# Second attention: the order of two TensorE steps changed, and the scaling of the row maxima moved from VectorE to ScalarE

## The chip, the cores and the metric

The kernel runs on one NeuronCore of a Trainium2 chip. The metric is the device time of one execution in microseconds. Five engines work side by side and wait for one another through semaphores: TensorE (PE, with its weight loads PEld), VectorE (DVE), ScalarE (ACT), GpSimd (POOL) and SyncE (SP), which issues most DMAs.

## The reference, cut to what matters

The program is a two-layer decoder over 128 sequences of 64 tokens of width 128. The change touches one of its stages, the self-attention of the second layer. It attends across the batch: for each of the 64 token positions ("columns") the 128 sequences are rows, with 16 heads of width 8, a bias key and value appended, and a relative position bias that a gate computed from the query scales.

```python
attn_weights = jnp.einsum('bth,bsh->bts', q, k)          # q scaled by hd**-0.5 / 32
gate = jax.nn.sigmoid((query_layer @ grep_w + grep_b).sum(-1, keepdims=True))
gate = (gate * grep_a).reshape(bsz * nh, tgt_len, 1)
attn_weights = attn_weights + gate * pb
probs = jax.nn.softmax(attn_weights, axis=-1)
attn = jnp.einsum('bts,bsh->bth', probs, v)
return attn @ out_w + out_b                              # then + x and a layernorm
```

## The kernel before, in words

The program runs its stages one after the other, with a barrier between them. `phase_attn1` is the stage in question. It handles 64 columns of 128 rows; four buffers of each kind let several columns be under way at once. `pipelined` writes the order of work out by hand: every engine walks the columns in the same rhythm, each column in four quarters (a = 0 to 3, four heads each), and in every quarter an engine runs a fixed list of steps that belong to different columns: `ahead2` and `ahead1` are the columns two and one further on, `column` the one whose scores are being made, `behind1` to `behind3` the ones before. The lists are the functions named `step`, one for each engine. An engine never leaves the order of its list, so a wait holds up all that stands behind it.

The way of a column: TensorE turns x (`turn_x`) and projects it (`project`, L1697 and L1698); VectorE adds the biases (L1894, L1896, L1900) and ends the column's rows with `choose` (L1905); ScalarE and GpSimd split them into float16 high and low parts (L1804 to L1806, L1660, L1661); VectorE transposes all in 32x32 blocks (`turn_rows`, L1910, 1.8 us each); GpSimd makes the gate's right-hand side (L1632); TensorE makes gates and values (`gates_and_values`, 4 matmuls on L1707 and 16 on L1709); ScalarE starts the sigmoid and copies the values (L1811, L1813, L1814), VectorE inverts it (L1915), GpSimd scales it (L1638).

Then come the quarters. TensorE makes four heads of scores (L1719). VectorE's `bias` adds the gated positions while it copies the scores out (L1930), takes the row maxima of four heads (L1932), and multiplies these by -SCALE (L1934, 128x4 values, after a wait for L1932's own end). ScalarE's `exps` waits for that, and computes exp(SCALE * score + negmax) for each head (L1820). TensorE turns the result (`turn`, L1727), ScalarE copies it (L1825), TensorE weighs the values (`weigh`, 32 matmul records on L1746), ScalarE copies that (`copy_weighed`, L1833), and TensorE combines the parts (`combine`, L1756 and L1758). VectorE's `normalise` (L1940, L1942) waits for `combine`; it stands in quarter 0 behind `bias` of the column two further on. Then TensorE turns and projects the result (L1764, L1768), VectorE adds x and takes the statistics (L1948, L1950, L1953), GpSimd makes the power (L1622 to L1627) and ScalarE the norm (L1848) and the store.

In quarter 0 TensorE's list reads: scores(column, 1), turn(behind1, 2), turn_x(ahead2), gates_and_values(ahead1), combine(behind2). In quarter 1 it goes on with project(ahead2), scores(column, 2), turn(behind1, 3) and turn_attn(behind2). In quarters 2 and 3 it has scores(column, 3), turn(column, 0), output(behind2), then scores(ahead1, 0), turn(column, 1), turn_last(behind1), weigh(behind1).

ScalarE's list in quarter 0 reads: copy_weighed, exps(behind1, 3), copy_turned, place_last, copy_x, gates_and_values, norm; then exps(column, 0) in quarter 1, exps(column, 1) and high_parts in quarter 2, exps(column, 2) in quarter 3.

Of the kernel before, what the change touches and what calls it, by code (L numbers as in the profile page):

```python
# [9 lines left out]
ACT = mybir.ActivationFunctionType  # L10
ALU = mybir.AluOpType
AX = mybir.AxisListType.X
# [1470 lines left out]
def phase_attn1(nc, w, x3, x4):  # L1483
# [11 lines left out]
    SCALE = HD ** -0.5 / 32.0  # L1495
# [4 lines left out]
    with Phase(nc, "c") as ph:  # L1500
        def slots(name, shape, dt=F32):
            return [ph.sb(f"{name}{j}", shape, dt) for j in range(U)]
# [8 lines left out]
        sc, pT = slots("sc", [T, H, KEYS]), slots("pT", [T, H, T])  # L1511
        top, negmax, den = slots("top", [T, H]), slots("negmax", [T, H]), slots("den", [T, H])
# [9 lines left out]
        names = ("consts", "xT_ready", "xT_copied", "qvk_ready", "vlast_ready", "whole_ready", "high_ready", "rows_ready", "misc_ready", "gate_exp", "v_ready",  # L1522
                 "gate_done", "posg_ready", "scores_ready", "biased", "top_ready", "exp_ready", "pT_ready", "pT_copied", "last_placed", "kv_next_ready",
                 "lastT_ready", "lastT_copied", "pv_ready", "attn_ready", "attnT_ready", "attnT_copied", "out_ready", "x_biased_ready", "x_added", "mv_ready",
                 "rstd_ready", "offset_ready", "x4_ready", "own_front", "var_ready", "gate_added", "gate_ready", "last_bias_ready", "gate_inverted", "own_quarters", "own_back", "waited", "pool_waited", "low_ready", "rhs_ready", "chosen_ready", "weighed_ready", "weighed_copied")
        (consts, xT_ready, xT_copied, qvk_ready, vlast_ready, whole_ready, high_ready, rows_ready, misc_ready, gate_exp, v_ready,
         gate_done, posg_ready, scores_ready, biased, top_ready, exp_ready, pT_ready, pT_copied, last_placed, kv_next_ready,
         lastT_ready, lastT_copied, pv_ready, attn_ready, attnT_ready, attnT_copied, out_ready, x_biased_ready, x_added, mv_ready,
         rstd_ready, offset_ready, x4_ready, own_front, var_ready, gate_added, gate_ready, last_bias_ready, gate_inverted, own_quarters, own_back, waited, pool_waited, low_ready, rhs_ready, chosen_ready, weighed_ready, weighed_copied) = (ph.sem(n) for n in names)

        def nth(it, j):
            return U * it + j + 1

        def quarter(it, j, a):
            return Q * U * it + Q * j + a + 1

        def slot(j):
            return j % U
# [27 lines left out]
        def run(part, position, *more):  # L1566
            if position is not None:
                part(*position, *more)
# [15 lines left out]
        with nc.Block() as block:  # L1584
            @block.sync
            def _(sp):
                def body(it):
                    for j in range(U):
                        if not is_first(it):
                            sp.wait_ge(xT_ready, nth(it, j) - U)  # L1590
                        sp.dma_start(x_sb[j][:], x3_tokens[bass.ds(U * it + j, 1)].rearrange("o r i d -> (o r) i d")).then_inc(loaded[j], 16)
                        if not is_first(it):
                            sp.wait_ge(x_biased_ready, nth(it, j) - U)
                        sp.dma_start(x_rows[j][:], x3_rows[bass.ds(U * it + j, 1)].rearrange("o h t d -> (o h) t d")).then_inc(rows_loaded[j], 16)
                peeled(nc.sync, steps, body)
                for j in range(U):
                    sp.wait_ge(stored[j], 16 * (steps + 1))
# [85 lines left out]
            def _(pe):  # L1683
# [86 lines left out]
                def step(a, ahead2, ahead1, column, behind1, behind2, behind3):  # L1770
                    if a == 0:
                        run(scores, column, 1)
                        run(turn, behind1, 2)
                        run(turn_x, ahead2)
                        run(gates_and_values, ahead1)
                        run(combine, behind2)
                    if a == 1:
                        run(project, ahead2)
                        run(scores, column, 2)
                        run(turn, behind1, 3)  # L1780
                        run(turn_attn, behind2)
                    if a == 2:
                        run(scores, column, 3)
                        run(turn, column, 0)
                        run(output, behind2)
                    if a == 3:
                        run(scores, ahead1, 0)
                        run(turn, column, 1)
                        run(turn_last, behind1)
                        run(weigh, behind1)  # L1790
                pipelined(nc.tensor, step)

            @block.scalar
            def _(act):
# [21 lines left out]
                def exps(it, j, a):  # L1816
                    s = slot(j)
                    act.wait_ge(top_ready, quarter(it, j, a))
                    for h in range(4 * a, 4 * a + 4):
                        last = nc.scalar.activation(sc[s][:, h, :], sc[s][:, h, :], ACT.Exp, bias=negmax[s][:, h:h + 1], scale=SCALE)  # L1820
                    last.then_inc(exp_ready, 1)
# [55 lines left out]

            @block.vector
            def _(dve):
                front_own, quarters_own, back_own = Own(dve, own_front), Own(dve, own_quarters), Own(dve, own_back)  # L1880
                dve.wait_ge(consts, 1)
                for j in range(U):
                    nc.vector.tensor_copy(gate_rhs[j][:, :, 0:4], w["gate_w"][:].unsqueeze(1).to_broadcast([P, 4, 4]))
# [3 lines left out]
                def place(it, j):  # L1887
                    return U * it + j
# [32 lines left out]
                    nc.vector.tensor_tensor(sc[s][:, :, T].rearrange("p (a i) -> p i a", a=4), gates_part(1), by_gate(last_bias[s]), ALU.add).then_inc(gate_done, 1)  # L1921

                def bias(it, j, a):
                    s, own, hs = slot(j), quarters_own, slice(4 * a, 4 * a + 4)
                    if a == 0:
                        own.step(place(it, j))
                        dve.wait_ge(gate_done, nth(it, j))
                    dve.wait_ge(scores_ready, quarter(it, j, a))
                    dve.wait_ge(posg_ready, quarter(it, j, a))
                    nc.vector.tensor_tensor(sc[s][:, hs, 0:T], sbank[a % 2][:], posg[a][:], ALU.add).then_inc(biased, 1)  # L1930
                    dve.wait_ge(biased, quarter(it, j, a))
                    m = own.mark(nc.vector.tensor_reduce(top[s][:, hs], sc[s][:, hs, :], AX, ALU.max))  # L1932
                    own.wait(m)
                    nc.vector.tensor_scalar(negmax[s][:, hs], top[s][:, hs], -SCALE, None, ALU.mult).then_inc(top_ready, 1)  # L1934

                def normalise(it, j):
                    s, own = slot(j), back_own
# [17 lines left out]
                def step(a, ahead2, ahead1, column, behind1, behind2, behind3):  # L1955
                    if a == 0:
                        run(bias, column, 0)
                        run(normalise, behind2)
                    if a == 1:
                        run(bias, column, 1)  # L1960
                        run(invert_gates, ahead1)
                        run(project, ahead2)
                    if a == 2:
                        run(bias, column, 2)
                        run(last_score, ahead1)
                        run(choose, ahead2)
                        run(add_x, behind2)
                    if a == 3:
                        run(bias, column, 3)
                        run(turn_rows, ahead2)  # L1970
# [841 lines left out]
def program(nc, d, out):  # L2812
# [10 lines left out]
    with Phase(nc, "all") as top:  # L2823
        ident = make_ident(nc, top)
        with Phase(nc, "w0") as ph:
            w = setup_l0(nc, ph, inputs("attn0"), ident)
            with Phase(nc, "parts") as parts:
                xT_parts = [parts.sb(f"xT_{part}", [D, TOK], F16) for part in ("high", "low")]
                phase_max(nc, d["xT"], w["Wkp"], w, xT_parts)
                phase_performer(nc, w, d["x"], xT_parts, y1)  # L2830
            phase_feed_forward0(nc, w, d["x"], y1, x1)
        with Phase(nc, "w2") as ph:
            w = setup_cross0(nc, ph, inputs("cross0"), ident)
            phase_cross0(nc, w, x1, d["ctx"], d["ctxT"], x3)
        with Phase(nc, "w3") as ph:
            w = setup_attn1(nc, ph, inputs("attn1"), ident)
            phase_attn1(nc, w, x3, x4)
        with Phase(nc, "w4") as ph:
            w = setup_cross1(nc, ph, inputs("cross1"), ident)
            phase_cross1(nc, w, x4, d["ctxT"], x5, x5T, coefT)  # L2840
        with Phase(nc, "w5") as ph:
            w = setup_moe(nc, ph, inputs("moe"), ident)
            phase_moe(nc, w, x5, x5T, coefT, out)
# [71 lines left out]
```

## Time and profile before

| | us |
|---|---|
| median of three runs | 4170.33 (4169.57 to 4176.07) |
| the profiled execution's own time | 4170.93 |
| its span | 4169.2 |
| the stage in question, from the profile's lines | about 1640 to 2515 |

Over the whole span TensorE is busy 85% of the time, VectorE 75%, ScalarE 56%, GpSimd 44%. These are averages over the stages with different limits; what follows reads the one stage. The span and the own time differ by 1.7 us of start and end. An instruction's row gives its start from the beginning of the span and its length. Two instructions of one engine that do not need each other overlap by about 0.1 us in the records, so start-to-start distances are what adds up.

### The profile page before, as it was taken

To read this page: it belongs to the slowest core of one execution; us is meant where nothing else is said; L and a number is where in the kernel's file an instruction comes from. 1 tells how busy PE (TensorE), PEld (TensorE's weight loads), DVE (VectorE), ACT (ScalarE), POOL (GpSimd) and SP (SyncE) were. 2 spreads that over 40 slices of the span, in tenths; PEclk is the share of its full clock that TensorE was granted. 3 is DMA by queue.
4 is the path that set the end of the run, shared out by engine and by line. 5 is a ranking of instruction groups with operands and counts; after the bars stand their busy time and mean duration, and the time that the engine had idled before them with its cause. 6 is when DMAs were issued, how large, how long until landed. Compare 5 with 4: busy or idle time off the path is not lost. (4 is left out here: it accounts for less than half of the span.)

```text
span 4169.2 us, 92263 instructions
## 1 busy us (share of the span) xinstructions
PE 3546.1 (85%) x30947; PEld 2307.8 (55%) x30947; DVE 3141.0 (75%) x6490; ACT 2355.2 (56%) x5257; POOL 1843.5 (44%) x2322
## 2 busy tenths in 40 slices
PE   6899999997776853899889996887849999999998
PEld 3466666664445752666666665776724444444443
DVE  6677777775664653888888885888858888888887
ACT  1455555555663431777777775556545555555555
POOL 1000000002654642655565662222237878787876
PEclk9999999998886775777776768889869999999999
DMA  2000000001112212000000001222165656655663
GB/s 79 7 9 10 10 10 10 10 10 31 54 38 76 68 37 41 16 13 15 14 14 15 14 9 49 57 55 56 46 159 141 135 136 139 134 142 134 138 135 88
DMA packets 279447, 245.68 MB, mean 59 GB/s; under 512 B 57832, under 2 KB 205196, under 8 KB 279180
## 3 DMA queue, kind: packets, MB, share of 16 engines
q1 hardware_dynamic: 270092, 239.77, 23.7%
q10 hardware_dynamic: 9216, 4.20, 0.4%
q8 instruction: 70, 1.15, 0.1%
q14 instruction: 69, 0.57, 0.0%
HBM read 210.34 MB, written 33.55 MB: 58 GB/s over the span
## 5 line engine op out<-in xcount | busy, mean ns | idle before, releaser
L2647 POOL TENSOR_TENSOR d_hidden<-d_gated,d_upper 128x512 f32<-128x512 f32 x528 | 801.9, 1544 | 228.7 <-DVE d_upper L2756 101.1
L2763 DVE TENSOR_TENSOR d_h_low<-d_hidden,d_h_high 128x512 f16<-128x512 f32 x528 | 540.8, 1024 | 118.8 <-ACT d_h_high L2723 117.5
L2717 ACT ACTIVATE d_gated<-d_g 128x512 f32<-128x512 f32 x528 | 315.2, 597 | 461.9 <-PE d_u L2663 461.9
L750 POOL MEMSET f_minus_half<- 128x4 f32 x1 | 0.1, 101 | 864.4 <-POOLq L37 864.4
L2756 DVE TENSOR_TENSOR d_upper<-d_u,d_coef 128x512 f32<-128x512 f32 x512 | 349.1, 682 | 29.3 <-DMA d_coef<-coefT 10.9
L2723 ACT ACTIVATE d_h_high<-d_hidden 128x512 f16<-128x512 f32 x528 | 328.4, 622 | 8.2 <-POOL d_hidden L2647 8.2
L1820 ACT ACTIVATE c_sc<-c_sc,c_negmax 128x129 f32<-128x129 f32 x1024 | 326.2, 393 | 11.8 <-issue 7.6
L1648 POOL TENSOR_TENSOR c_posg<-w_pos,c_gate 128x512 f32<-128x512 f32 x256 | 266.0, 1039 | 0.0
L2661 PE MATMUL d_g<-d_x_high,w_Wg_high 128*128 128x512 f16 x528 | 200.5, 380 | 72.0 <-POOL d_x_low L2640 36.8
L1825 ACT ACTIVATE c_pT<-c_turned 128x512 f32<-128x512 f32 x256 | 149.7, 585 | 153.8 <-PE c_turned L1727 153.6
L1727 PE MATMUL c_turned<-all_ident,c_sc 128*128 128x128 f32 x1024 | 229.7, 365 | 6.4 <-ACT c_sc L1820 5.9
L2661 PE MATMUL d_o<-d_h_high,w_Wd_high 128*128 128x512 f16 x528 | 200.1, 379 | 2.0 <-ACT d_h_high L2723 1.6
L2661 PE MATMUL d_u<-d_x_high,w_Wu_high 128*128 128x512 f16 x528 | 200.6, 380 | 0.0
L2663 PE MATMUL d_g<-d_x_low,w_Wg_high 128*128 128x512 f16 x528 | 200.6, 380 | 0.0
L2662 PE MATMUL d_g<-d_x_high,w_Wg_low 128*128 128x512 f16 x528 | 200.6, 380 | 0.0
L2662 PE MATMUL d_u<-d_x_high,w_Wu_low 128*128 128x512 f16 x528 | 200.4, 380 | 0.0
L2663 PE MATMUL d_u<-d_x_low,w_Wu_high 128*128 128x512 f16 x528 | 200.4, 379 | 0.0
L2662 PE MATMUL d_o<-d_h_high,w_Wd_low 128*128 128x512 f16 x528 | 200.1, 379 | 0.0
L2663 PE MATMUL d_o<-d_h_low,w_Wd_high 128*128 128x512 f16 x528 | 200.1, 379 | 0.0
L1727 PEld LDWEIGHTS c_turned<-all_ident,c_sc 128*128 128x128 f32 x1024 | 149.1, 183 | 63.3 <-issue 50.8
L1932 DVE TENSOR_REDUCE c_top<-c_sc 128x4 f32<-128x516 f32 x256 | 176.9, 691 | 8.8
L1719 PE MATMUL c_scores<-c_rows 24*128 24x128 f16 x1024 | 160.8, 290 | 19.4 <-DVE c_sc L1930 19.3
(409 smaller groups left out, 9909.5 us busy)
## 6 DMA issues: line engine op xcount, KB each, us to landing
d_coef<-coefT SPq DMA_DIRECT2D x256, 512.0 KB, 7.6
d_cT<-in_ctxT SPq DMA_DIRECT2D x128, 64.0 KB, 2.0
mx_x<-in_xT SPq DMA_DIRECT2D x16, 256.0 KB, 2.7
b_x<-in_x SPq DMA_DIRECT2D x64, 64.0 KB, 1.8
y<-b_y SPq DMA_DIRECT2D x64, 64.0 KB, 1.6
f_y<-y SPq DMA_DIRECT2D x16, 256.0 KB, 3.2
f_x<-in_x SPq DMA_DIRECT2D x16, 256.0 KB, 3.7
x<-f_res SPq DMA_DIRECT2D x16, 256.0 KB, 2.4
```

The source lines that it names most:

```text
L1648: nc.gpsimd.tensor_tensor(posg[a][:], w["pos"][:, hs, :], gate[s][:, hs].unsqueeze(2).to_broadcast([T, 4, T]), ALU.mult).then_inc(posg_rea ...
L1727: last = nc.tensor.transpose(tbank[a % 2][:, i, :], sc[slot(j)][:, 4 * a + i, 0:T], w["ident"][:])
L1820: last = nc.scalar.activation(sc[s][:, h, :], sc[s][:, h, :], ACT.Exp, bias=negmax[s][:, h:h + 1], scale=SCALE)
L1932: m = own.mark(nc.vector.tensor_reduce(top[s][:, hs], sc[s][:, hs, :], AX, ALU.max))
L2647: nc.gpsimd.tensor_tensor(hidden[b][:], gated[b][:], upper[b][:], ALU.mult).then_inc(h_ready, 1)
L2661: nc.tensor.matmul(out, weights[0], high, start=start, stop=False)
L2662: nc.tensor.matmul(out, weights[1], high, start=False, stop=False)
L2663: return nc.tensor.matmul(out, weights[0], low, start=False, stop=stop)
L2717: nc.scalar.activation(gated[b][:], ps_g[i][:], ACT.Silu, scale=1.0 / W_SCALE).then_inc(silu_ready, 1)
L2723: nc.scalar.activation(h_high[b][:], hidden[b][:], ACT.Copy).then_inc(h_high_ready, 1)
L2756: nc.vector.tensor_tensor(upper[b][:], ps_u[i][:], coef[c % CBUFS][:, u % CU, :], ALU.mult).then_inc(upper_ready, 1)
L2763: nc.vector.tensor_tensor(h_low[b][:], hidden[b][:], h_high[b][:], ALU.subtract).then_inc(h_low_ready, 1)
```

## The change

Two edits in `phase_attn1`.

TensorE, quarter 0: `combine(behind2)` now runs ahead of `gates_and_values(ahead1)`.

VectorE no longer multiplies the maxima by -SCALE: L1934 and the wait in front of it are gone, and L1932 itself releases ScalarE. ScalarE does the multiplication at the head of `exps`, one small copy for each quarter, and waits for its end before the four exponentials. A semaphore for VectorE's own quarters is replaced by one for ScalarE's.

```diff
                         run(turn_x, ahead2)
+                        run(combine, behind2)
                         run(gates_and_values, ahead1)
-                        run(combine, behind2)
...
                 def exps(it, j, a):
                     s = slot(j)
                     act.wait_ge(top_ready, quarter(it, j, a))
+                    nc.scalar.activation(negmax[s][:, 4 * a:4 * a + 4], top[s][:, 4 * a:4 * a + 4], ACT.Copy, scale=-SCALE).then_inc(negmax_ready, 1)
+                    act.wait_ge(negmax_ready, quarter(it, j, a))
                     for h in range(4 * a, 4 * a + 4):
...
                     dve.wait_ge(biased, quarter(it, j, a))
-                    m = own.mark(nc.vector.tensor_reduce(top[s][:, hs], sc[s][:, hs, :], AX, ALU.max))
-                    own.wait(m)
-                    nc.vector.tensor_scalar(negmax[s][:, hs], top[s][:, hs], -SCALE, None, ALU.mult).then_inc(top_ready, 1)
+                    nc.vector.tensor_reduce(top[s][:, hs], sc[s][:, hs, :], AX, ALU.max).then_inc(top_ready, 1)
```

## Rows read from the trace of the kernel before

**Rows 1.** The page: the span.

```profile
span 4169.2 us, 92263 instructions
```

**Rows 2.** Stretches: us; busy PE, PEld, DVE, ACT, POOL; clock; DMA. Then L1910 alone.

```profile
1668.05:2486.05 818.00, 740.15 (x6208) 546.98 (x6200) 700.08 (x1440) 596.54 (x1982) 488.38 (x899) 0.71 0.05 14
...
1668.05:2000.00 331.95, 44.97 (x25) 0.73 0.05 14
2000.00:2486.05 486.05, 62.93 (x35) 0.71 0.05 14
```

**Rows 3.** Waits from 1700 to 2500: total us, times, longest.

```profile
DVE c_den L1940 <- PE c_back L1758: 70.8, 59, 1.8
```

**Rows 4.** Timeline, VectorE in a short column: start us, us, instruction.

```profile
2008.96 1.80 DVE L1910 STREAM_TRANSPOSE c_rows<-c_padded 128x1568 f16<-128x1568 f16 x1
...
2011.37 0.69 DVE L1932 TENSOR_REDUCE c_top<-c_sc 128x4 f32<-128x516 f32 x1
...
2012.10 0.40 DVE L1934 TENSOR_SCALAR c_negmax<-c_top 128x4 f32<-128x4 f32 x1
...
2013.15 0.26 DVE L1940 RECIPROCAL c_den<-c_back 128x16 f32<-128x16 f32 x1 [0.65 <-PE c_back L1758]
...
2014.36 0.69 DVE L1932 TENSOR_REDUCE c_top<-c_sc 128x4 f32<-128x516 f32 x1
...
2015.17 0.24 DVE L1915 RECIPROCAL c_gate<-c_gate 128x16 f32<-128x16 f32 x1
...
2015.33 0.49 DVE L1894 TENSOR_TENSOR c_whole<-c_front,w_qvk_b 128x384 f32<-128x384 f32 x1
...
2020.41 0.69 DVE L1932 TENSOR_REDUCE c_top<-c_sc 128x4 f32<-128x516 f32 x1
...
2021.14 0.84 DVE L1934 TENSOR_SCALAR c_negmax<-c_top 128x4 f32<-128x4 f32 x1
...
2021.89 1.80 DVE L1910 STREAM_TRANSPOSE c_rows<-c_padded 128x1568 f16<-128x1568 f16 x1
```

**Rows 5.** Timeline, the other engines around quarter 0.

```profile
2010.73 0.41 PE L1690 MATMUL c_front<-all_ident,c_x 128*128 128x128 f32 x1
...
2011.80 0.49 PE L1756 MATMUL c_back<-c_vlast_rows,c_lastT 128*128 128x144 f32 x2
...
2012.13 0.98 PE L1758 MATMUL c_back<-w_picked,c_weighed 128*128 128x36 f32 x8
...
2020.91 1.04 POOL L1648 TENSOR_TENSOR c_posg<-w_pos,c_gate 128x512 f32<-128x512 f32 x1
...
2021.98 0.59 ACT L1833 ACTIVATE c_weighed<-c_back 128x512 f32<-128x512 f32 x1
...
2024.11 0.29 PE L1707 MATMUL c_misc<-c_gate_rhs,c_rows 128*128 128x8 f16 x4 [1.52 <-POOL c_gate_rhs L1632]
```

**Rows 6.** Timeline, the long column that follows.

```profile
2027.22 0.26 DVE L1940 RECIPROCAL c_den<-c_back 128x16 f32<-128x16 f32 x1 [1.79 <-PE c_back L1758]
...
2029.50 0.56 DVE L1894 TENSOR_TENSOR c_whole<-c_front,w_qvk_b 128x384 f32<-128x384 f32 x1
...
2036.35 1.80 DVE L1910 STREAM_TRANSPOSE c_rows<-c_padded 128x1568 f16<-128x1568 f16 x1
```

**Rows 7.** Timeline, TensorE's next `gates_and_values`, one column after that of rows 5.

```profile
2038.50 0.30 PE L1707 MATMUL c_misc<-c_gate_rhs,c_rows 128*128 128x8 f16 x4
```

**Rows 8.** Busy time by stretch, three stretches with their granted clock (PEclk).

```profile
2024.65:2038.30 13.65, 13.65 (x91) 10.15 (x90) 10.93 (x24) 8.60 (x28) 7.33 (x15) 0.50 0.05 14
2011.11:2024.11 13.00, 10.82 (x104) 7.91 (x104) 11.69 (x25) 10.39 (x36) 8.22 (x16) 0.87 0.05 15
...
2017.82:2021.23 3.41, 3.41 (x41) 2.42 (x38) 3.12 (x10) 2.37 (x8) 1.72 (x4) 0.50 0.00 0
```

**Rows 9.** Timeline, ScalarE: a small activation that waits for the one before.

```profile
2011.98 0.29 ACT L1811 ACTIVATE c_gate<-c_misc,w_neg_gate_b 128x16 f32<-128x16 f32 x1
...
2012.30 0.21 ACT L1813 ACTIVATE c_gate<-c_gate 128x16 f32<-128x16 f32 x1
```

More of the change, by code:

```diff
@@ L1524, in phase_attn1 @@
                  "lastT_ready", "lastT_copied", "pv_ready", "attn_ready", "attnT_ready", "attnT_copied", "out_ready", "x_biased_ready", "x_added", "mv_ready",
-                 "rstd_ready", "offset_ready", "x4_ready", "own_front", "var_ready", "gate_added", "gate_ready", "last_bias_ready", "gate_inverted", "own_quarters", "own_back", "waited", "pool_waited", "low_ready", "rhs_ready", "chosen_ready", "weighed_ready", "weighed_copied")
+                 "rstd_ready", "offset_ready", "x4_ready", "own_front", "var_ready", "gate_added", "gate_ready", "last_bias_ready", "gate_inverted", "negmax_ready", "own_back", "waited", "pool_waited", "low_ready", "rhs_ready", "chosen_ready", "weighed_ready", "weighed_copied")
         (consts, xT_ready, xT_copied, qvk_ready, vlast_ready, whole_ready, high_ready, rows_ready, misc_ready, gate_exp, v_ready,
@@ L1528, in phase_attn1 @@
          lastT_ready, lastT_copied, pv_ready, attn_ready, attnT_ready, attnT_copied, out_ready, x_biased_ready, x_added, mv_ready,
-         rstd_ready, offset_ready, x4_ready, own_front, var_ready, gate_added, gate_ready, last_bias_ready, gate_inverted, own_quarters, own_back, waited, pool_waited, low_ready, rhs_ready, chosen_ready, weighed_ready, weighed_copied) = (ph.sem(n) for n in names)
+         rstd_ready, offset_ready, x4_ready, own_front, var_ready, gate_added, gate_ready, last_bias_ready, gate_inverted, negmax_ready, own_back, waited, pool_waited, low_ready, rhs_ready, chosen_ready, weighed_ready, weighed_copied) = (ph.sem(n) for n in names)
         def nth(it, j):
@@ L1879, in _ @@
             def _(dve):
-                front_own, quarters_own, back_own = Own(dve, own_front), Own(dve, own_quarters), Own(dve, own_back)
+                front_own, back_own = Own(dve, own_front), Own(dve, own_back)
                 dve.wait_ge(consts, 1)
@@ L1923, in bias @@
                 def bias(it, j, a):
-                    s, own, hs = slot(j), quarters_own, slice(4 * a, 4 * a + 4)
+                    s, hs = slot(j), slice(4 * a, 4 * a + 4)
                     if a == 0:
-                        own.step(place(it, j))
                         dve.wait_ge(gate_done, nth(it, j))
```

## The prediction, made before the changed kernel was run

> **What bounds the kernel now.** I read the page first, for the span [rows 1], and found the stage by its lines. It is one stage of several, and the barrier behind it passes on whatever it gains or loses, so only its own rhythm matters. The busy time of its steady part comes next [rows 2]: VectorE runs L1910 once a column, 25 + 35 = 60 times in 818.0 us, so a column takes 13.63 us. In it TensorE is busy 740.15/60 = 12.3 us, VectorE 11.7, ScalarE 9.9, GpSimd 8.1. The granted clock is 0.71 on average, a mix of the levels 1.2 GHz (0.5) and 2.4 GHz (1.0): 42% of the time at the upper one.
>
> No engine is full, so the bound is a chain. The view of waits shows one wait of VectorE for another engine that counts: L1940 for TensorE's `combine`, 70.8 us in 59 times, 1.20 us a column [rows 3]. The timeline shows VectorE working without another such gap. From L1910 to L1910 a short column takes 2021.89 - 2008.96 = 12.93 us with 0.65 us of that wait [rows 4]; the column after it takes 2036.35 - 2021.89 = 14.46 with 1.79 us of it [rows 6]. Half the columns are of either kind, which makes the mean.
>
> Why `combine` is late shows on TensorE's side: it stands behind `gates_and_values`, which can only begin when L1910 and then GpSimd's L1632 are done. TensorE sits idle for that, 1.52 us before L1707 at 2024.11 [rows 5], although all that `combine` needs (ScalarE's L1833) was finished at 2021.98 + 0.59 = 2022.57. So the loop that sets the pace is: L1910, L1632, gates and values, `combine`, `normalise`, the rest of VectorE's list, L1910 again.
>
> **First edit, `combine` first.** Nothing is added; on TensorE two steps change places and SP's and GpSimd's queues are not touched. `combine` now waits for L1833 alone and takes 13.11 - 11.80 = 1.31 us at the upper clock level [rows 5]; in the long column it took until 2027.2 [rows 6]. VectorE wants it at the end of L1932, 2011.37 + 0.69 = 2012.06, or 3.10 us after L1910 started. From 2022.6 it would be done at 2023.9 to 2024.1, two microseconds after L1910's start: the wait of L1940 is gone in the columns that begin like this one. In the short column TensorE reached this place only at about 2011.0 (`turn_x` at 2010.73 for 0.41 us [rows 5]), so `combine` ends at 2012.3, 0.2 to 0.3 us late. At the lower clock level it takes about 1.1 us more, by the two waits (1.79 against 0.65 us [rows 4, 6]). What stands behind it pays: `gates_and_values` starts when `combine` ends, at worst 1.3 us later. Of that, VectorE's L1915 notices nothing, since it is not due until 2.9 us after L1940's place, and the transfer of the wait goes to `project`, next on TensorE, which L1894 needs.
>
> **Second edit, VectorE's part.** L1934 costs differently by the quarter. In quarter 0 L1932 ends at 2012.06 and L1934 at 2012.50: 0.44. In quarter 1 L1932 ends at 2015.05 and L1915 starts at 2015.17: 0.12, and quarter 2 repeats it. In quarter 3 L1932 ends at 2021.10 and L1910 starts at 2021.89: 0.79 [rows 4]. The long ones end when a GpSimd instruction ends: L1648 at 2020.91 + 1.04 = 2021.95, L1934 at 2021.98 [rows 5]. All of it lies on VectorE's chain. Together 0.44 + 0.12 + 0.12 + 0.79 = 1.47 us, and with the wait of 0.65 the short column shrinks from 12.93 to 10.8 us. That is VectorE's floor. I cost the next instructions at no new stall, since none of their kinds (reduce, transpose, reciprocal) shows varying lengths.
>
> **Second edit, ScalarE's part.** Four small copies a column. The trace of before has no 128x4 copy here; the nearest are L1813 (128x16, 0.21 us), and the pair L1811 and L1813, where the second waits for the first: 0.32 start to start for a length of 0.29 [rows 9]. Neighbours that don't wait overlap by nearly 0.1 us (L1915 ends at 2015.41, L1894 starts at 2015.33 [rows 4]). From below a copy costs 0.21 - 0.08 = 0.13 us, from above 0.21 + 0.03 = 0.24; since the exponentials must wait for its end I take 0.24, 4 x 0.24 = 1.0 us a column. ScalarE goes from 9.9 to 10.9 us a column. The Trainium skill, "ScalarE: Activation LUTs", section "What ACT_TABLE_LOAD costs", gives 186 ns plus 0.833 ns an element for such an instruction, an estimate of 0.19 us. By that figure the four would be 0.1 us a column cheaper than the 0.21 of the row; the small difference stays in the range.
>
> ScalarE waits long enough in a column (13.63 - 9.9 = 3.7 us) to take 1.0 in, as long as a column is longer than about 11.0 us. Queued behind the new wait are the exponentials, `copy_turned` and, from quarter 3, L1833. Who waits: `turn` and `combine` on TensorE. Against that, L1932 releases ScalarE 0.2 to 0.9 us sooner than L1934 did, so the exponentials do not come later.
>
> **What is late next.** By walking the two columns: the short one becomes 10.8 + 0.2 = 11.0. In the long one `combine` begins about 1.5 us sooner (TensorE's idle time is filled), so `project`, for whose end L1894 started at 2029.50 [rows 6], ends about 2028.0; VectorE wants it at L1910 plus the distance of the short column less what is gone in between, 2015.33 - 2008.96 - 0.44 - 0.65 - 0.12 = 5.16, so at 2027.05. It waits 0.9: 11.7 us. The mean of the two is 11.35.
>
> TensorE may not follow, and this decides. With the clock at 0.50 it was busy without a gap for 13.65 us (2024.65 to 2038.30) [rows 8], and from gates to gates, 2024.11 [rows 5] to 2038.50 [rows 7], took 14.39: a column at the lower level costs 14.4 us. The stretch 2011.11 to 2024.11 holds 10.82 us of work, 3.41 of it at 0.50 (2017.82 to 2021.23) [rows 8]. These 3.41 do 3.41/14.39 = 0.237 of a column, the other 7.41 us the remaining 0.763: a column at the upper level costs 9.7. With today's 42% of the time at the upper level a TensorE that never waits needs 1/(0.42/9.7 + 0.58/14.39) = 12.0 us. With 50% it is 11.6, with 60% 11.15.
>
> I expect the share to rise a little, since the idle gap before L1707 goes away (the clock fell at 2024.65, right behind it), and some waits to stay: 11.8 us a column. **The sum:** 60 x (13.63 - 11.8) = 110 us, and about 3 us for the columns at the two ends. The profiled execution's own time is 4170.9 us, 0.6 above the median of the three runs; 4170.9 - 113 = 4058 us.
>
> **Rivals.**
>
> 1. The clock stays up. The forecast then meets the floors of VectorE (10.8) and ScalarE (10.9 plus a stall or two): 11.0 to 11.2 us, 60 x 2.5 + 4 = 154 us less, 4017. For it: the gap before L1707 goes. Against: the clock stood at 0.50 through 13.65 us of unbroken work [rows 8], so a busy TensorE alone does not raise it here. The rule that speaks for this rival is in the Trainium skill, "TensorE: Matmul & The Clock Gate", section "Why this matters for your kernels": keep TensorE busy and free of long gaps and it holds full clock. By that rule the time would be this rival's 4017; the row just named disagrees. Chance 0.2.
>
> 2. The waits only move. `combine` waits for L1833 behind a fuller ScalarE, `gates_and_values` and `project` wait behind `combine`, and L1894 inherits most of L1940's wait. VectorE keeps the 1.47 us of L1934 at best, and half of it if TensorE's chain is the tighter: 12.3 to 13.0 us a column, 40 to 80 us less, about 4110. For it: the order of the work ahead of `project` is the same sum as before. Against: 1.5 us of idle time in half of the columns. Chance 0.2.
>
> 3. Slower: the clock stays at the lower level. The upper stretches of today begin near `weigh` and last through `combine` and `project`; if TensorE now waits for L1833 where it used to go on with `gates_and_values`, they may not come. Then a column costs 14.4 us: 60 x 0.76 = 46 us more, 4217. It decides once 1/(w/9.7 + (1 - w)/14.39) exceeds 13.63, that is w under 0.12 or a mean granted clock under 0.56 against today's 0.71. Chance 0.06.
>
> 4. No change, if both engines' chains happen to lengthen by what is cut: 0.03.
>
> **How the numbers follow.** The forecast itself, 11.4 to 12.2 us a column, has 0.51. Together with rivals 1 and 2 that is 0.91 for faster by over 0.2% (8 us, about what a measurement of this kernel can tell from no change), 0.03 for within it and 0.06 for slower. The range takes in rival 1 down to 10.8 us a column (60 x 2.8 = 170, 4001, cut to 4006 because two engines would have to be full at once) and most of rival 2 (12.8 us: 50 + 2, 4118).
>
> **What the profile will show.** No L1934; L1940's wait for L1758 down from 1.2 to under 0.4 us a column; the wait of L1707 for L1632 nearly gone, since `combine` fills it; a ScalarE copy of 0.2 us before each group of exponentials, its busy time up by about 1 us a column; new, larger waits of L1894 for L1698 and shorter ones of ScalarE's L1825. TensorE's busy share should rise from 0.90 towards 0.95. The forecast fails upward if the granted clock of the stage falls under 0.65 or if ScalarE's L1833 turns out to end later than TensorE's `turn_x` in most columns; it fails downward if the clock rises above 0.8.

## The result and the profile after

The changed kernel takes 4107.4 us (median of 4, 4105.8 to 4109.4) against 4172.2 for the kernel before on the same chip: a ratio of 0.984 (95% interval 0.983 to 0.985), 65 us less. The forecast was 4058. The change helps, by a little more than half of what was forecast.

The profiled execution has a span of 4104.0 us, 65.2 below the one before. Three intervals, read from first and last starts, and the rest say where that is from:

| us | before | after | |
|---|---|---|---|
| attention stage, first to last L1910 (L1912 after), 63 intervals | 849.9 | 747.4 | -102.5 |
| from there to the first hidden product of the last stage (L2647, L2646 after) | 601.4 | 603.8 | +2.4 |
| last stage, first to last hidden product | 1067.5 | 1098.0 | +30.5 |
| ahead of the attention stage's first L1910, and the end | 1650.4 | 1654.8 | +4.4 |

So the attention stage came close to what was forecast: 747.4/63 = 11.86 us a column with the short ones at its start, 727.00/61 = 11.92 in the steady part that the forecast of 11.8 was made for. A stage that the change does not touch gave 30 us back.

First the attention stage. Busy time by stretch of the changed kernel (its steady part; the columns as in [rows 2]):

```profile
1660.75:2387.75 727.00, 676.59 (x6242) 492.42 (x6246) 624.50 (x1215) 647.14 (x2254) 493.12 (x910) 0.79 0.06 16
```

The granted clock rose from 0.71 [rows 2] to 0.79, TensorE's busy share from 0.90 to 0.93. The waits of the same stretch, where [rows 3] had 70.8 us for VectorE's L1940:

```profile
ACT c_pT L1827 <- PE c_turned L1727: 55.6, 33, 2.2
...
DVE c_whole L1896 <- PE c_ahead L1698: 40.1, 33, 1.3
...
PE c_turned L1727 <- ACT c_sc L1822: 29.3, 66, 1.6
...
PE c_back L1756 <- ACT c_weighed L1835: 11.4, 32, 0.4
DVE c_den L1939 <- PE c_back L1758: 10.9, 28, 0.6
...
PE c_front L1697 <- ACT c_xT L1799: 9.3, 33, 0.5
...
PEld c_misc L1707 <- POOL c_gate_rhs L1632: 0.5, 1, 0.5
```

VectorE's wait for `combine` is 10.9 us in all; the wait for GpSimd's L1632 ahead of gates and values is down to 0.5 us, on one weight load. New is the wait of VectorE for `project` (L1896), 40.1 us, and TensorE now waits for ScalarE in three places: for the exponentials, for the copy of the weighed values and for the copy of the turned x. The first of these was small in the kernel before:

```profile
PE c_turned L1727 <- ACT c_sc L1820: 3.8, 15, 0.5
```

The lines of the groups show what ScalarE's copy costs by itself:

```profile
L1819 ACT ACTIVATE c_negmax<-c_top 128x4 f32<-128x4 f32 x244 | 48.3, 198 | 11.4 <-issue 9.3
```

That is 198 ns. It is near the prediction's estimate of 0.19 us from the Trainium skill, "ScalarE: Activation LUTs", section "What ACT_TABLE_LOAD costs". The timeline of a long column (12.8 us; they alternate with ones of 11.1) shows how the new waits hang together:

```profile
1993.47 0.66 PE L1727 MATMUL c_turned<-all_ident,c_sc 128*128 128x128 f32 x4 [0.37 <-ACT c_sc L1822]
...
1994.60 0.51 PE L1756 MATMUL c_back<-c_vlast_rows,c_lastT 128*128 128x144 f32 x2 [0.36 <-ACT c_weighed L1835]
...
1996.83 1.65 PE L1697 MATMUL c_front<-w_qvk_w,c_xT 128*128 128x384 f32 x2 [0.28 <-ACT c_xT L1799]
...
1998.27 1.06 PE L1698 MATMUL c_ahead<-w_qvk_w,c_xT 128*128 128x256 f32 x2
...
1999.37 0.56 DVE L1896 TENSOR_TENSOR c_whole<-c_front,w_qvk_b 128x384 f32<-128x384 f32 x1 [1.34 <-PE c_ahead L1698]
```

and its clock, in stretches of 1 us (PEclk is the third number from the end):

```profile
1995.00:1996.00 1.00, 1.00 (x17) 1.00 (x17) 0.84 (x3) 1.00 (x5) 1.00 (x3) 1.00 0.00 0
1996.00:1997.00 1.00, 0.72 (x18) 0.64 (x17) 0.97 (x3) 0.97 (x6) 1.00 (x3) 0.52 0.00 0
1997.00:1998.00 1.00, 1.00 (x2) 0.67 (x3) 0.97 (x3) 0.97 (x5) 0.70 (x1) 0.50 0.00 0
```

TensorE stands still for ScalarE for about 0.3 us three times, twice ahead of the fall of the clock to 1.2 GHz (0.50) at about 1996 and once behind it. `project` runs at the lower level, and VectorE waits 1.34 us for its end. ScalarE is busy in 0.97 to 1.00 of these stretches. That the stops ahead of the fall caused it is not shown; the experiments below come back to it.

Now the last stage. DMA queues of 700 us of its steady part, before:

```profile
q1 hardware_dynamic: 57527, 95.61, 60.7%
q8 instruction: 1, 0.02, 0.0%
```

and after:

```profile
q1 hardware_dynamic: 55520, 91.76, 58.4%
q14 instruction: 50, 0.41, 0.2%
q8 instruction: 2, 0.03, 0.0%
```

Before, the program's instructions were hardly fetched here; after, queue 14 moves 50 packets of them, in five groups that begin about 140 us apart (3252, 3394, 3534, 3674 and 3813 us). The waits of the same 700 us after have two that the view of before does not:

```profile
DVE d_upper L2755 <- issue: 28.5, 5, 6.8
ACT d_gated L2716 <- issue: 19.4, 4, 6.3
```

"issue" is time for which no other engine is answerable. It comes five and four times, each time beside one of the five groups of packets, once in a turn of the stage's loop. The timeline of one:

```profile
3259.86 0.60 ACT L2716 ACTIVATE d_gated<-d_g 128x512 f32<-128x512 f32 x1 [6.35 <-issue]
...
3261.22 0.69 DVE L2755 TENSOR_TENSOR d_upper<-d_u,d_coef 128x512 f32<-128x512 f32 x1 [6.76 <-issue]
...
3262.05 0.58 PE L2660 MATMUL d_g<-d_x_high,w_Wg_high 128*128 128x512 f16 x1 [5.16 <-DVE d_upper L2755]
...
3262.43 0.63 PE L2661 MATMUL d_g<-d_x_high,w_Wg_low 128*128 128x512 f16 x1
```

ScalarE and VectorE have nothing to execute for over 6 us, TensorE runs dry behind them (5.16 us) and works on at the lower clock level (0.63 us for a matmul that took 0.38).

### The profile page after: what moved, and what is told of

It reads as the page before. It is cut to its first block and busy times, and to the rows that moved or that the text cites. A ratio compares the mean times of both kernels' runs of the same rounds, so it can differ in the third digit from the quotient of the medians.

```text
span 4104.0 us, 92053 instructions
## 1 busy us (share of the span) xinstructions
PE 3493.4 (85%) x30947; PEld 2259.6 (55%) x30947; DVE 3056.2 (74%) x6234; ACT 2400.2 (58%) x5513; POOL 1842.5 (45%) x2322
## 5 line engine op out<-in xcount | busy, mean ns | idle before, releaser
L2646 POOL TENSOR_TENSOR d_hidden<-d_gated,d_upper 128x512 f32<-128x512 f32 x528 | 803.0, 1546 | 259.7 <-DVE d_upper L2755 126.9
L1727 PE MATMUL c_turned<-all_ident,c_sc 128*128 128x128 f32 x1024 | 211.6, 341 | 30.6 <-ACT c_sc L1822 30.6
L1727 PEld LDWEIGHTS c_turned<-all_ident,c_sc 128*128 128x128 f32 x1024 | 135.5, 169 | 91.4 <-ACT c_sc L1822 55.9
L1931 DVE TENSOR_TENSOR c_sc<-c_scores,c_posg 128x512 f32<-128x512 f32 x256 | 172.9, 676 | 0.5 <-issue 0.3
```

Of the source, the lines that this page charges most:

```text
L1727: last = nc.tensor.transpose(tbank[a % 2][:, i, :], sc[slot(j)][:, 4 * a + i, 0:T], w["ident"][:])
L2646: nc.gpsimd.tensor_tensor(hidden[b][:], gated[b][:], upper[b][:], ALU.mult).then_inc(h_ready, 1)
```

## The experiments

The theory: in the attention stage the loop through `combine` was the bound and is cut, and ScalarE's copies eat part of the gain through TensorE's clock. In the last stage the change moved the loop's code: ahead of it VectorE's program has 64 instructions fewer and ScalarE's 48 more (counted in the two programs). The rivals: `combine` first is worth nothing by itself; TensorE's own work is the bound; the last stage suffers from DMA contention or from when it begins.

The Trainium skill, "Runtime: NRT & Kernel Launch", section "Instruction fetch mechanics", says that an engine's instructions come in blocks of 256 into room for two (more for TensorE), and that a taken branch to a block not held stalls for a fetch. By that rule a loop of 312 instructions (VectorE's) or 341 (ScalarE's) needs two blocks or three, by where it begins. The packets on queue 14, 50 more of them in five groups, agree. Where a block ends in these programs was not read; the runs below move the loops and see what comes of it.

**The first edit alone.**

```diff
+                        run(combine, behind2)
                         run(gates_and_values, ahead1)
-                        run(combine, behind2)
```

> The kernel of before with the first edit alone: combine ahead of gates and values. Theory: the loop L1910, gates, combine, normalise is cut, so L1940's wait (1.13 us a column) mostly goes, but L1934 stays on VectorE's chain with 1.47 us a column. The short column becomes 12.93 - 0.65 + 0.2 = 12.4 us, the long one about 12.8 to 13.2: the attention stage saves 60 x 0.8 to 1.1 = 50 to 65 us. VectorE's and ScalarE's instruction streams are those of before, so the last stage (mixture of experts) shows no bursts of instruction fetches and keeps its 1067 us from its first to its last hidden product; the whole gains 50 to 65 us. Rival: the order gains nothing by itself since project then makes VectorE wait (L1894): less than 20 us. Rival on the last stage: if it lengthens here too, by 30 us, the cause is not where its code lies.

4094.7 us, ratio 0.982 (0.980 to 0.984). That is faster than both edits together: the slowest of its runs took 4097.0 us, the fastest with both 4105.8. The attention stage takes 769.8 us, 80.1 less, more than expected; the last stage 1068.5. Most columns take 12.18 us, in which VectorE waits for no other engine: its floor with L1934. The waits of VectorE in the stage, and the fetches over the whole run:

```profile
DVE c_whole L1900 <- DVE c_next_kv L1896: 9.6, 59, 0.5
DVE c_mv L1953 <- DVE c_bn L1950: 9.1, 58, 0.2
...
DVE c_whole L1894 <- PE c_ahead L1698: 4.0, 7, 0.7
```

```profile
q14 instruction: 69, 0.57, 0.0%
```

That is VectorE waiting for itself, 4.0 us for `project` against 40.1 with both edits, and as few fetches as before.

**The second edit alone** (the diff of the change without the two lines above).

> The second edit alone: ScalarE scales the maxima, combine stays behind gates and values. Theory: VectorE's chain between normalise and the next L1910 loses 0.12 + 0.12 + 0.79 us; the 0.44 of quarter 0 lies under the wait for combine and gives nothing. A column falls by 1.0 us, 60 us in the stage. VectorE's and ScalarE's code in front of the last stage is as long as in the changed kernel, so the last stage should lengthen by 30 us as there and show some ten instruction fetches every 140 us; the whole gains 25 to 35 us. Rival: TensorE's combine comes later because ScalarE has 1 us more to do, and the stage gains under 25 us. Rival on the last stage: it keeps its 1067 us here, and the lengthening belongs to the moved combine or to chance.

4164.1 us, ratio 0.9985 (0.997 to 1.000), 7.5 us less than the kernel before on its chip where 25 to 35 were expected. The attention stage takes 809.2 us, 40.7 less where 60 were expected. VectorE's wait for `combine` is longer:

```profile
DVE c_den L1939 <- PE c_back L1758: 113.6, 60, 2.9
```

It was 71.5 us in 60 times before. Of the 42 us more, 26 (0.44 us a column) had been foreseen; the other 16 are most of what is missing. The last stage takes 1094.1 us with 121 packets on queue 14, although `combine` was not moved: its lengthening comes with this edit. Of the two, 80.1 + 40.7 = 120.8 us of gain, 102.5 are left when both are made.

**The changed kernel with 64 instructions put back on VectorE's queue.**

```diff
             def _(dve):
+                for n in range(64):
+                    dve.sem_inc(dve_pads, 1)
                 for n, (k, c) in enumerate(work):
```

> The changed kernel with 64 semaphore increments put on VectorE's queue in the set-up ahead of the last stage, where it waits for the weights. This puts its loop in the last stage back to the place (instruction 3139 of its stream) that it has in the kernel before; ScalarE's loop stays 48 instructions later than before. Theory: each engine fetches instructions in blocks; a loop that lies across one block more has to be fetched again in each of its turns. If VectorE's shift by 64 is the cause, the bursts go and the last stage falls from 1098 to about 1068 us, the whole from 4107 to about 4077. If ScalarE's shift by 48 is the cause, nothing changes. If both, some of the 30 us. The rival that the lengthening comes from DMA contention or from when the stage begins expects no change, within 5 us.

4088.9 us, ratio 0.981 (0.979 to 0.982); last stage 1083.3, queue 14 with 95 packets (120 after, 69 before). VectorE's wait is gone, ScalarE's stays:

```profile
ACT d_gated L2719 <- issue: 19.2, 4, 5.8
```

**With 208 more on ScalarE's queue** (the same two lines with `act`, ahead of its weight copies).

> As the last, with 208 more increments on ScalarE's queue at the same place (48 + 208 = 256, one whole block), so that both loops of the last stage lie as they do before, up to whole blocks. Theory: the last stage takes about 1068 us again, no bursts of fetches, the whole 4072 to 4080, perhaps some us more where the increments themselves are not hidden behind the loads (208 of them at 0.05 us are 10 us). The rival (contention, or the time at which the stage begins) expects 4107 or, with the increments, more.

4084.2 us, ratio 0.979 (0.977 to 0.981). Last stage 1067.6 us, 72 packets: half of the 30 us was VectorE's place and half ScalarE's. The stretch between the stages grew from 603.8 to 611.9, the price of the increments. That is 8.1 us, or 0.04 us each; no run had shown the 0.05 of the expectation before.

**84 instead of 208**, behind ScalarE's last weight copy (VectorE's 64 stay).

```diff
                     nc.scalar.activation(w[k][0][:, c:c + CHUNK, :], stage[n % BUFS][:], ACT.Copy, scale=W_SCALE).then_inc(high_ready, 1)
+                for n in range(84):
+                    act.sem_inc(act_pads, 1)
```

> The changed kernel with 64 semaphore increments on VectorE's queue ahead of the last stage, as before, and only 84 on ScalarE's, put behind its last weight copy of the set-up, where VectorE is still at work. Theory: a loop of 341 instructions needs three blocks of 256 from some places and two from the others; 48 instructions of shift took ScalarE's out of the good places, 84 more carry it past the block's edge just as 208 did. The last stage takes 1068 us, no bursts of fetches, and the stretch between the two stages 603 to 605 us instead of the 612 with 208 increments; the whole 4070 to 4080. Rival: only the very place of the kernel before is good, and the last stage takes some 1083 us as with VectorE's increments alone.

4078.1 us, ratio 0.977 (0.976 to 0.978); last stage 1067.7, 71 packets. So the one place of before is not the only good one, as loops that need two blocks from some places and three from others would have it. The stretch between was 610.2, so I was wrong that VectorE's work would hide the increments.

**The converse: the kernel before, shifted** (192 and 48 increments at the head of the same two queues).

> The converse: the kernel before, whose attention stage is left alone, with 192 semaphore increments on VectorE's queue and 48 on ScalarE's in the set-up ahead of the last stage. Up to whole blocks of 256 this puts both loops of the last stage where they lie in the changed kernel (192 is 256 - 64). Theory: the attention stage stays at 850 us, the last stage goes from 1067 to 1094 to 1098 us with bursts of fetches every 140 us (some 50 more packets on queue 14), the whole from 4171 to 4200, and a few us more where the increments are not hidden. Rival: the lengthening needs something else of the changed kernel, and the last stage stays at 1067 us.

4216.4 us, ratio 1.011 (1.009 to 1.013), where 4200 and a few more were expected. The attention stage takes 849.3 us, the last one 1099.7, with 122 packets on queue 14. Nothing of the change is in this kernel but where the code lies. The stretch between took 618.0, 16.6 more; in the kernels without such increments it varies from 597.7 to 603.8.

The rival of contention, or of when the stage begins, is out. Over all kernels of this document the last stage took 1067.3 to 1068.5 us in the six whose two loops lie as before or in an equally good place, which began it between 2940 and 3088 us, and 1094.1 to 1099.7 in the four with both loops moved, which began it between 2951 and 3101. The one kernel with a single loop moved has the 1083.3.

**ScalarE's copies left out.**

```diff
-                    nc.scalar.activation(negmax[s][:, 4 * a:4 * a + 4], top[s][:, 4 * a:4 * a + 4], ACT.Copy, scale=-SCALE).then_inc(negmax_ready, 1)
-                    act.wait_ge(negmax_ready, quarter(it, j, a))
...
-                        last = nc.scalar.activation(sc[s][:, h, :], sc[s][:, h, :], ACT.Exp, bias=negmax[s][:, h:h + 1], scale=SCALE)
+                        last = nc.scalar.activation(sc[s][:, h, :], sc[s][:, h, :], ACT.Exp, bias=minus_half[:], scale=SCALE)
```

ScalarE waits once for the constants at the stage's start, and VectorE's 64 increments are in, so that both loops of the last stage lie as before (it takes 1067.6 us).

> The changed kernel without ScalarE's small copies: the exponentials take a constant as their bias (the scaling of the maxima and the subtraction are left out), one wait at the stage's start is added, and VectorE's 64 increments keep the last stage's loops in place. It tells what the copies cost. ScalarE loses 4 x 0.24 = 1.0 us of work a column. Theory: in the changed kernel VectorE's wait for project (0.67 us a column) comes from TensorE standing idle for ScalarE's exponentials and its copy of the weighed values, after which the clock falls and project runs at the lower level. With ScalarE 1 us shorter, TensorE is not held up: 11.0 to 11.4 us a column against 11.86 (747.4/63), attention stage 695 to 720 us. Rival: TensorE's own work at the mixed clock is the bound, and the stage stays within 10 us of 747.

A single run, 4023.3 us. The attention stage takes 703.4 us, 44.0 less than with the copies: 11.17 us a column. VectorE's wait for `project` falls from 40.1 to 14.7 us, and the clock is up:

```profile
1656.00:2339.00 683.00, 635.26 (x6270) 459.11 (x6270) 616.42 (x1215) 606.86 (x2009) 494.11 (x911) 0.89 0.06 17
```

0.89 against 0.79. TensorE does the same work in 635.3 us of busy time instead of 676.6. ScalarE still waits for the maxima; what is gone with the copies is its wait for the end of each, so the 44 us are the price of both.

What the expectation said of the way from the copies to the clock does not hold. TensorE waits for the exponentials for as long as with the copies, and more often:

```profile
PE c_turned L1727 <- ACT c_sc L1822: 30.1, 94, 1.4
...
PE c_back L1756 <- ACT c_weighed L1835: 16.2, 47, 0.4
```

With the copies it was 29.3 us in 66 times and 11.4 in 32. Only its wait for the copy of the turned x, 9.3 us in 33 times, is gone. The higher clock is shown; why it is higher stays open.

**`project`'s second half left out** behind the first column (keys and values of the following row are missing; the first half now gives the signal).

```diff
-                    nc.tensor.matmul(front[:, 0:3 * D], xT[s][:, 0:T], w["qvk_w"][:].rearrange("p a e -> p (a e)"), start=True, stop=True)
-                    nc.tensor.matmul(ahead[:, 0:2 * D], xT[s][:, AHEAD:T + AHEAD], w["qvk_w"][:, 1:3, :].rearrange("p a e -> p (a e)"),
-                                     start=True, stop=True).then_inc(qvk_ready, 1)
+                    if is_early(it, j, 1):
+                        nc.tensor.matmul(ahead[:, 0:2 * D], xT[s][:, 0:T], w["qvk_w"][:, 1:3, :].rearrange("p a e -> p (a e)"), start=True, stop=True)
+                    nc.tensor.matmul(front[:, 0:3 * D], xT[s][:, 0:T], w["qvk_w"][:].rearrange("p a e -> p (a e)"), start=True, stop=True).then_inc(qvk_ready, 1)
```

> The changed kernel with TensorE's second projection (L1698, 1.06 us at the lower clock level, 0.6 at the upper) left out after the first column, so keys and values of the following row are missing; all else is there. Theory: project's end is what VectorE waits for in every second column (1.34 us), so the wait falls by about 1 us there, 11.3 to 11.5 us a column, the stage 710 to 725 us. Rival 1: TensorE then idles more and its clock falls further, and the stage gains under 10 us. Rival 2: ScalarE is the bound, also under 10 us. The last stage keeps its bursts of fetches, 1098 us.

A single run, 4065.1 us. The attention stage takes 712.4 us, 35.0 less, 11.31 a column; the clock is 0.80 as with the work in (0.79), and the last stage keeps its 1098.2. VectorE's wait for the end of `project` falls from 40.1 to 9.5 us, so that end does bind the long columns, and leaving its work out hardly changes the clock. Less of TensorE's work and less of ScalarE's each shorten the column: no single engine is the bound there.

**The scaling on GpSimd.**

```diff
+                def scale_top(it, j, a):
+                    s, hs = slot(j), slice(4 * a, 4 * a + 4)
+                    pool.wait_ge(top_ready, quarter(it, j, a))
+                    pool.sem_inc(pool_waited, 1)
+                    nc.gpsimd.tensor_scalar(negmax[s][:, hs], top[s][:, hs], -SCALE, None, ALU.mult).then_inc(negmax_ready, 1)
...
+                    run(scale_top, column, a)
                     if a == 3:
                         run(power, behind2)
```

ScalarE then waits for `negmax_ready` alone. VectorE's 64 increments are in here too, and ScalarE's program is as long as before, so both loops of the last stage lie as before.

> The changed kernel with the scaling of the maxima on GpSimd instead of ScalarE, at the end of each of its quarters, and VectorE's 64 increments ahead of the last stage. ScalarE has its old 9.9 us a column, VectorE the 10.8 of the changed kernel, GpSimd gets four more instructions of 0.2 to 0.3 us (8.1 to 9.2 us a column). The maxima are ready 1.5 us or more before ScalarE comes for them, so GpSimd's queue should not delay it. Theory: close to the kernel without copies, 11.0 to 11.4 us a column, the whole at 4035 to 4055 us, faster than both kernels. Rival: GpSimd's wait for the maxima holds up the gated positions behind it (L1648, 1.04 us each), VectorE waits for these, and the column takes 12 us or more.

4030.6 us (4020.9 to 4035.3), ratio 0.9655 (0.964 to 0.967), outside and below the expected 4035 to 4055, and faster than both kernels. The kernel to compare it with has ScalarE's copies and both loops put back, 4078.1 us. The attention stage takes 706.9 us (11.22 a column), the last 1067.3. Busy time by stretch, and two of its waits:

```profile
1661.80:2348.30 686.50, 633.59 (x6270) 454.84 (x6270) 616.93 (x1215) 606.26 (x2009) 544.08 (x1155) 0.91 0.06 17
```

```profile
DVE c_sc L1936 <- POOL c_posg L1648: 14.7, 51, 0.5
...
DVE c_whole L1901 <- PE c_ahead L1705: 12.8, 19, 1.1
```

The clock is at 0.91. The feared wait of VectorE for the gated positions is there, but 14.7 us in all.

## Why the prediction was right, and where it fell short

**The bound and the first edit: right.** The loop through gates and values, `combine` and `normalise` set the pace; taking `combine` out of it removed most of VectorE's wait (70.8 to 10.9 us). What it is worth alone I put too low, in the expectation of that run: I had the short column of that edit at 12.4 us and the long one at 12.8 to 13.2, and most came out at 12.18. TensorE, no longer idle ahead of L1707, was given the upper clock level more often (0.77 against 0.71).

**VectorE's part of the second edit: right in size.** Columns in which VectorE hardly waits take 12.18 us with L1934 (the first edit alone) and 10.62 to 10.82 without it (the kernels without ScalarE's copies), 1.36 to 1.56 us less where 1.47 was forecast.

**ScalarE's part: the length right, its price wrong.** The copy takes 0.198 us, within the bounds of 0.13 and 0.24. But "ScalarE waits long enough in a column (13.63 - 9.9 = 3.7 us) to take 1.0 in, as long as a column is longer than about 11.0 us" failed. The column is longer than that, ScalarE is busy 647.1/61 = 10.6 us of its 11.92, and still 44 us of the stage hang on the copies. The slack was read in a column of 13.6 us. In the shorter one TensorE waits for ScalarE's results, and with the copies its granted clock is 0.79 instead of 0.89; the runs do not show by which path the copies lower it. The sign of failure that the prediction named, L1833 later than TensorE's `turn_x` in most columns, came in about half of them (32 waits in 61).

**TensorE's capacity: right in the sum.** The formula gave 11.6 to 12.0 us for an upper share of 42 to 50%; the clock of 0.79 is a share of 58%, for which it gives 11.2, and the rest of the 11.92 is waits. Two errors of about half a microsecond each offset one another, and that 11.8 came so near is in part luck. By the walk through the columns the short one should have taken 11.0 us and the long one 11.7; they take 11.1 and 12.8. The rule of the Trainium skill, "TensorE: Matmul & The Clock Gate", section "Why this matters for your kernels", to keep TensorE busy and free of long gaps, did not come true for this kernel. The clock of before stayed at the lower level through unbroken work [rows 8], and the clock of the changed kernel fell at 1996 although TensorE had not stopped for longer than 0.50 us since 1984.

**Where the 48 us went.** Forecast -113, measured -65. The attention stage gave 102.5 of the 113, 10.5 too few. The other 37 us went outside it, 30.5 of them in the last stage. That the measured time is almost the 4110 of rival 2 is chance: that rival had columns of 12.3 to 13.0 us, and they take 11.9. The step that failed is the first one: "the barrier behind it passes on whatever it gains or loses, so only its own rhythm matters". A change of the number of instructions in VectorE's and ScalarE's programs moves the code of every stage behind it, and here that cost 30.5 us in the last stage. The term was missing altogether. It belongs to the second edit: alone, that edit gains 40.7 us in the attention stage and loses 1094.1 - 1067.5 = 26.6 in the last. It is also why both edits together are slower than the first alone: 22.4 us better in the attention stage (769.8 - 747.4), 29.5 worse in the last (1098.0 - 1068.5).

The 4.4 us ahead of the stage and at the end are not explained. The first L1910 starts between 1633.4 and 1641.5 us in all these kernels with no pattern by edit, so I take them, unproven, for what varies between executions.

## What to carry to other kernels

Slack read from a profile belongs to the period in which it was read: when the loop that set the pace is cut, work moved to the engine that had time falls into a shorter period. TensorE's granted clock can then also be lower than without the moved work, as it was here (0.79 against 0.89). Before moving work, ask which engine has room at the new period; here it was GpSimd, 40.5 us better in the stage than ScalarE (706.9 against 747.4). After an edit that changes how many instructions an engine's program has, compare the stages that were not touched and the packets of the instruction queue: a loop may have slid to a place from which part of it is fetched again in every turn, and some idle instructions in a set-up put it back (here 64 and 84, which cost about 6 us of the 30 they saved).

## What the runs showed of the hardware that was not expected

A loop's place in its instruction stream was worth about 3 us for each of the two engines at each of the five groups of fetches: for 312 instructions on VectorE 14.7 us in the stage (1098.0 to 1083.3), for 341 on ScalarE another 15.7 (1083.3 to 1067.6), with about 50 packets on queue 14 in all. The engines themselves stand still for longer, up to 6.76 us at a time, so not all of it lengthens the stage. A semaphore increment is not free even in a set-up stage: 192 and 48 at the head of two queues lengthened the stretch between the stages from 601.4 to 618.0 us, while 64 on VectorE's cost nothing that can be seen (603.3 against 603.8).
